# Splitting the q and k projections head by head on ScalarE and VectorE instead of with DMAs, in a fused attention and FP4 feed-forward layer on one core

## The reference

```python
q = split_heads(x @ Wq.T); k = split_heads(x @ Wk.T); v = split_heads(x @ Wv.T)   # x here is layernorm(x)
sim = jnp.einsum('bhid,bhjd->bhij', q, k) * DIM_HEAD ** -0.5
attn = safe_softmax(sim)              # exp(s - max) / (sum + 1e-10)
out = jnp.einsum('bhij,bhjd->bhid', attn, v)
x = x + (out.transpose(0, 2, 1, 3).reshape(B, N, INNER) @ Wo.T + bo)
# feed-forward: both operands of every product are quantised to FP4 in blocks of 16
h = silu(fp4_linear(layernorm(x), w_gate)) * fp4_linear(layernorm(x), w_up)
x = x + fp4_linear(h, w_down)
```

## Time and profile before

| | before |
|---|---|
| median of three runs | 1707.32 us |
| profiled execution, its own time | 1707.32 us |
| its span in the trace | 1705.4 us |
| TensorE (PE) busy | 1529.4 us, 90% |
| VectorE (DVE) busy | 1307.2 us, 77% |
| GpSimd (POOL) busy | 1241.8 us, 73% |
| ScalarE (ACT) busy | 1133.5 us, 66% |
| granted TensorE clock, mean | 0.955 |
| q and k staging DMAs | 384, of 128 KB each, 2.3 to 2.4 us from issue to landing |

### The profile page before, as it was taken

One profiled execution on the slowest core, in us unless ns is written; L12 is line 12 of the kernel. 1 busy time (PEld: TensorE's weight loads), 2 busy tenths in 40 slices (PEclk: granted clock), 3 DMA queues, 4 the chain that ended last, 5 costly groups with the idle time before them and its releaser, 6 DMA issues.

```text
span 1705.4 us, 35322 instructions
## 1 busy us (share of the span) xinstructions
PE 1529.4 (90%) x13828; PEld 1045.6 (61%) x13828; DVE 1307.2 (77%) x2313; ACT 1133.5 (66%) x2094; POOL 1241.8 (73%) x1369
## 2 busy tenths in 40 slices
PE   3898999999899999999999999999999999999965
PEld 2466666666666666666666666666666666666644
DVE  6677876666787788888787887787877887887767
ACT  2577777777676666676666676666676766676633
POOL 3588788888777777777777777777777777777743
PEclk8799999999999999999999999999999999999977
DMA  6110111111111111111110111111111111111000
GB/s 150 38 39 20 35 30 39 37 42 39 30 40 40 38 25 33 25 40 40 39 28 23 32 41 40 39 24 26 33 40 40 38 28 25 29 40 40 2 4 12
DMA packets 46852, 59.77 MB, mean 35 GB/s; under 512 B 8864, under 2 KB 22112, under 8 KB 46688
## 3 DMA queue, kind: packets, MB, share of 16 engines
q1 hardware_dynamic: 46688, 57.52, 14.4%
HBM read 4.80 MB, written 2.10 MB: 4 GB/s over the span
## 4 chain that ended last, share of the span: by engine, by line
PE 66%; DVE 25%; POOL 4%; ACT 3%; issue 2%; DMA 0%; SPq 0%; DVEq 0%; ACTq 0%; POOLq 0%
PE ob L560 19%; PE sm L516 10%; PE st L534 10%; PE st L532 10%; DVE negm L822 6%; PE mb L461 5%; PE mb L477 3%; DVE qv L974 3%; ACT probs L644 2%; POOL p_low L400 2%; DVE q_small L970 2%; PE mb L1073 2%; DVE qv L986 2%; PE mb L466 2%; PE mb L472 2%
## 5 line engine op out<-in xcount | busy, mean ns | idle before, releaser
L400 POOL TENSOR_TENSOR p_low<-probs 128x512 f16<-128x512 f32 x1024 | 1084.8, 1068 | 354.2 <-ACT probs L644 349.3
L644 ACT ACTIVATE probs<-st,lift,exp_scale 128x512 f32<-128x512 f32 x1024 | 793.0, 775 | 312.9 <-PE st L534 292.8
L822 DVE TENSOR_REDUCE negm<-sm 128x1 f32<-128x1024 f32 x512 | 624.0, 1219 | 167.0 <-PE sm L516 166.7
L516 PE MATMUL sm<-k_hh,q_hl 128*128 128x512 f16 x1024 | 316.6, 392 | 100.5 <-DVE negm L822 91.6
L534 PE MATMUL st<-q_hm,k_l 66*128 66x512 f16 x1024 | 400.5, 391 | 0.0
L532 PE MATMUL st<-q_hl,k_hh 128*128 128x512 f16 x1024 | 399.6, 390 | 0.0
L560 PEld LDWEIGHTS ob<-v,p_low 128*128 128x128 f16 x4096 | 283.5, 99 | 129.2 <-issue 10.1
L560 PEld LDWEIGHTS ob<-v,probs 128*128 128x128 bf16 x4096 | 281.8, 99 | 128.9 <-issue 12.1
L560 PE MATMUL ob<-v,p_low 128*128 128x129 f16 x4096 | 325.8, 223 | 2.0 <-POOL p_low L400 2.0
L560 PE MATMUL ob<-v,probs 128*128 128x129 f16 x4096 | 323.0, 222 | 0.2
L658 ACT ACTIVATE oscl<-ob,rden 128x128 f32<-128x128 f32 x512 | 158.0, 363 | 53.5 <-DVE rden L812 53.5
(11 more groups left out here) (157 smaller groups left out, 1560.7 us busy)
## 6 DMA issues: line engine op xcount, KB each, us to landing
k_hh<-k_high SPq DMA_DIRECT2D x128, 128.0 KB, 2.3
k_l<-k_low SPq DMA_DIRECT2D x64, 128.0 KB, 2.3
q_hl<-q_high SPq DMA_DIRECT2D x64, 128.0 KB, 2.3
q_hm<-q_high SPq DMA_DIRECT2D x64, 128.0 KB, 2.4
q_hl<-q_low SPq DMA_DIRECT2D x64, 128.0 KB, 2.4
x<-x SPq DMA_DIRECT2D x4, 512.0 KB, 7.2
q_hm<-m_high SPq DMA_DIRECT2D x128, 1.0 KB
q_hm<-m_low SPq DMA_DIRECT2D x128, 1.0 KB
```

Source lines behind the costliest of these rows:

```text
L400: return pool.tensor_tensor(p_low[b][:, j, :], p, p.bitcast(BF16)[:, 1::2], ALU.subtract)
L516: pe.matmul(sm[:, s % 2, :], q_hl[n][:, t * P:(t + 1) * P], k_hh[n][:, (s % 2) * 512:(s % 2 + 1) * 512], start=True, stop=True).then_inc(s ...
L644: nc.scalar.activation(probs[k % 2][:, s, :], st[s % 2][:, :], ACT.Exp, bias=lift[:, 0:1], scale=exp_scale[:, head, pair:pair + 1]).then_i ...
L822: nc.vector.tensor_reduce(negm[k % 2][:, s // 2:s // 2 + 1], sm[:, :, :].rearrange("p a n -> p (a n)"), AX.X, ALU.max, negate=True).then_i ...
```

## The change

The staging tiles `q_parts` and `k_parts` go. ScalarE writes each head's high part from its 64 rows of the bank straight to its place (`q_hl` or `k_hh`, rows 0 to 63), in two instructions of 64 x 512 where one of 128 x 512 stood. VectorE writes each head's low part straight to its place (`q_hl` rows 64 to 127, or `k_l1` rows 0 to 63), also in two instructions. Four DMAs a round are left: two copy k high to rows 64 to 127 of `k_hh`, and two copy q high to `q_hm`. The first `sm` of the new pair waits for the low parts and for the k copies, and the wait for the q copies stands a round later, at slot 0 of the pair's own scores. The semaphores count eight steps a round in place of four.

```diff
-        q_parts = [sb(f"q_{part}", [P, N], F16) for part in ("high", "low")]
-        k_parts = [sb(f"k_{part}", [P, N], F16) for part in ("high", "low")]
...
-                    wait(sp, s_hi, 4 * g + 2)
+                    wait(sp, s_hi, 8 * g + 4)
                     for h in range(2):
-                        high = k_parts[0][h * DH:(h + 1) * DH, :]
-                        sp.dma_start(k_hh[n + h][0:DH, :], high).then_inc(s_dk, 16)
-                        sp.dma_start(k_hh[n + h][DH:P, :], high).then_inc(s_dk, 16)
-
-                    wait(sp, s_lo, 4 * g + 2)
-                    for h in range(2):
-                        sp.dma_start(k_l1[n + h][0:DH, :], k_parts[1][h * DH:(h + 1) * DH, :]).then_inc(s_dk, 16)
+                        sp.dma_start(k_hh[n + h][DH:P, :], k_hh[n + h][0:DH, :]).then_inc(s_dk, 16)
...
-                    wait(sp, s_hi, 4 * g + 4)
+                    wait(sp, s_hi, 8 * g + 8)
                     for h in range(2):
-                        high = q_parts[0][h * DH:(h + 1) * DH, :]
-                        sp.dma_start(q_hl[n + h][0:DH, :], high).then_inc(s_dq, 16)
-                        sp.dma_start(q_hm[n + h][0:DH, :], high).then_inc(s_dq, 16)
-
-                    wait(sp, s_lo, 4 * g + 4)
-                    for h in range(2):
-                        sp.dma_start(q_hl[n + h][DH:P, :], q_parts[1][h * DH:(h + 1) * DH, :]).then_inc(s_dq, 16)
+                        sp.dma_start(q_hm[n + h][0:DH, :], q_hl[n + h][0:DH, :]).then_inc(s_dq, 16)
...
                         if k == 2 and s == 0:
-                            wait(pe, s_dk, 96 * (g + 1))
-                            wait(pe, s_dq, 96 * (g + 1))
+                            wait(pe, s_lo, 8 * (g + 1))
+                            wait(pe, s_dk, 32 * (g + 1))
...
+                            if slot == 0:
+                                wait(pe, s_dq, 32 * g)
...
-                    nc.scalar.activation(k_parts[0][:, cols], bank[:, :], ACT.Copy,
-                                         scale=k_scale[:, g % PAIRS:g % PAIRS + 1]).then_inc(s_hi, 1)
+                    for h in range(2):
+                        nc.scalar.activation(k_hh[2 * (1 - q) + h][0:DH, cols], bank[h * DH:(h + 1) * DH, :], ACT.Copy,
+                                             scale=k_scale[h * DH:(h + 1) * DH, g % PAIRS:g % PAIRS + 1]).then_inc(s_hi, 1)
...
-                    nc.vector.tensor_tensor(q_parts[1][:, cols], bank[:, :], q_parts[0][:, cols], ALU.subtract
-                                            ).then_inc(s_lo, 1)
+                    for h in range(2):
+                        n = 2 * (1 - q) + h
+                        wait(dve, s_hi, 8 * g + 4 + 2 * c + h + 1)
+                        nc.vector.tensor_tensor(q_hl[n][DH:P, cols], bank[h * DH:(h + 1) * DH, :], q_hl[n][0:DH, cols],
+                                                ALU.subtract).then_inc(s_lo, 1)
...
-                    nc.vector.scalar_tensor_tensor(out=k_parts[1][:, cols], in0=bank[:, :],
-                                                   scalar=k_scale[:, g % PAIRS:g % PAIRS + 1], in1=k_parts[0][:, cols],
-                                                   op0=ALU.mult, op1=ALU.subtract).then_inc(s_lo, 1)
+                    for h in range(2):
+                        n = 2 * (1 - q) + h
+                        wait(dve, s_hi, 8 * g + 2 * c + h + 1)
+                        nc.vector.scalar_tensor_tensor(out=k_l1[n][0:DH, cols], in0=bank[h * DH:(h + 1) * DH, :],
+                                                       scalar=k_scale[h * DH:(h + 1) * DH, g % PAIRS:g % PAIRS + 1],
+                                                       in1=k_hh[n][0:DH, cols], op0=ALU.mult, op1=ALU.subtract
+                                                       ).then_inc(s_lo, 1)
```

More of the change, by code:

```diff
@@ L251, in taken @@
             if name[0] in "qk":
-                return s_lo, 4 * g + (0 if name[0] == "k" else 2) + c + 1
+                return s_lo, 8 * g + (0 if name[0] == "k" else 4) + 2 * c + 2
             if name[0] == "v":
@@ L602, in take @@
                     wait(act, mb_ready[JOBS[m][1]], ready)
-                    nc.scalar.activation(q_parts[0][:, cols], bank[:, :], ACT.Copy).then_inc(s_hi, 1)
+                    for h in range(2):
+                        nc.scalar.activation(q_hl[2 * (1 - q) + h][0:DH, cols], bank[h * DH:(h + 1) * DH, :], ACT.Copy
+                                             ).then_inc(s_hi, 1)
                 elif name[0] == "k":
@@ L771, in take @@
                 if name[0] == "q":
-                    wait(dve, s_hi, 4 * g + 2 + c + 1)
-                    nc.vector.tensor_tensor(q_parts[1][:, cols], bank[:, :], q_parts[0][:, cols], ALU.subtract
-                                            ).then_inc(s_lo, 1)
-                elif name[0] == "k":
-                    wait(dve, s_hi, 4 * g + c + 1)
-                    nc.vector.scalar_tensor_tensor(out=k_parts[1][:, cols], in0=bank[:, :],
-                                                   scalar=k_scale[:, g % PAIRS:g % PAIRS + 1], in1=k_parts[0][:, cols],
-                                                   op0=ALU.mult, op1=ALU.subtract).then_inc(s_lo, 1)
+                    for h in range(2):
[3 more added lines that the diff above has]
+                                                ALU.subtract).then_inc(s_lo, 1)
+                elif name[0] == "k":
+                    for h in range(2):
+                        n = 2 * (1 - q) + h
[4 more added lines that the diff above has]
+                                                       ).then_inc(s_lo, 1)
                 elif name[0] == "m":
```

## The result

The changed kernel takes 1755.04 us (median of 4 runs, 1754.06 to 1755.81) against 1706.46 us for the kernel before on the same chip (4 runs, 1705.01 to 1707.89). The ratio is 1.0284 [1.0268, 1.0299]: 48.6 us slower, where 36.7 us were forecast. In the trace the span grew from 1705.4 to 1755.0 us.

A forecast was written before the change was run, and what follows sets the result against it. TensorE was taken to bound the kernel (busy 90% of the span, 66% of the chain). Terms of 5.4, 4.4, 29.9 and -3 us made +36.7 us on 1707.32: forecast 1744 us, range 1732 to 1756.

The forecast's parts named there:

- The price of a half: On VectorE and ScalarE, 64 x 512 costs what 128 x 512 did, 0.75 or 0.69 us; row changes add 0.12 us.
- Rival A: VectorE's overlap survives the change of rows, so k1 starts only 0.25 us late: +7.5 us, 1715 us; chance 22%.
- rival D: Two halves cost at most 0.4 us more than the whole and round 0 gains 4 us: 1703 us; chance 7%.
- Steps 1 and 2: On TensorE, k1 waits for `m_low`, 0.5 us, and t0 for q0's low part, 0.4 more: 0.9 us a plain round.
- Step 3: Feed-forward rounds: reduction at (1, 1) 1.59 us late past quantisation at (1, 0), score pair waits 0.4 us; 1.3 a round.
- Step 4: Rounds 3 and 4: TensorE already waits for the reduction at (1, 1), so its lateness goes straight through; 2.2 us each.
- step 5: Round 0: the first score pair no longer waits for two q copies and starts earlier; 3 us gained.
- Rival B: New short stops lower the clock of feed-forward rounds by two hundredths more: 23 x 1.0 us on top, 1767 us; chance 10%.
- ScalarE: costed at nothing: ScalarE's added halves, at most 2.8 us a round, are covered by idle time: nothing, or 2.4 us without that cover.
- The moved waits and the DMAs: Later q-copy wait and the wait at (2, 0) cost nothing; removing eight hidden DMAs gives nothing in the steady state.

The follow-up runs named there:

- experiments 9 and 10: Hidden tile's first quantisation piece cut, reciprocal and product moved to (3, 6): first in the kernel before, 1642.39 us; then in the changed kernel, 1707.65 us.
- experiment 7: Kernel before with ScalarE's and VectorE's conversions in halves of 64 x 512 into the staging tiles, all twelve copies kept: 1751.15 us, ratio 1.0272.

## Why the prediction was right, and where its size was off

**The price of a half: right.** 749 and 689 ns, and row changes as taken: `m_low` begins 1.56 us after k0's low part (forecast 1.58), and 0.03 us after the pair's end; in the q pair the reduction begins 1.44 us after (forecast 1.46). The column split shows that it is the change of rows: there the follower begins 0.08 us before the end. The rule of the Trainium skill ("VectorE: DVE Perf Modes", section "Two Vector instructions with no wait between them") says which instructions are held; the trace agrees at each pair: the second half begins 0.03 us after the end of the first, in all 64 pairs of k halves and all 64 of q halves. Rival A is out by this, rival D by the durations.

**Steps 1 and 2: right.** 0.49 us at k1 (forecast 0.5), 0.97 in all (0.9), no further wait in a plain round; taking `m` ahead of k0 removed the first wait, though a plain round got back only 0.18 us of it. Rounds 5 to 8 gave 4.0 us for 3.6.

**Step 3: right place, size off by 1.1 us.** The reduction at (0, 7) was 1.63 us late (forecast 1.59). But the prediction passed this lateness on unchanged through the quantisation at (1, 0): "this one is 1.59 us late". In the traces the reduction at (1, 1) is 2.25 us late. The 0.62 us between are L980, 1331 ns for 712, because it now begins behind GpSimd's `p_low`; the step at (1, 2) adds 0.29. This makes a wait of 0.40 at (1, 2) that was not forecast, and a longer one at (1, 4). From k0's low part the pair at (1, 2) went from 11.43 to 13.01 us and that at (1, 4) from 14.58 to 16.99. With `p_low` cut short the step took 0.52 us, which shows the cause of its length; how much of the price is due to it alone was not isolated. So the term that was mis-sized is 22 x 1.3 = 28.6 us; at full clock it measured 21 x 2.41 and 1.0 for round 9, 51.6.

**Step 4 and step 5: right in size.** Rounds 1 to 4 gave 6.8 us for 6.2: rounds 1 and 2 together 3.0 for 1.8, round 3 1.3 and round 4 2.5 for 2.2 each. Round 0 gave 4.2 for 3. The first score pair began 3.2 us earlier, at 34.84 us (forecast near 34):

```profile
34.84 1.01 PE L502 MATMUL sm<-k_hh,q_hl 128*128 128x512 f16 x2 [2.94 <-DVE q_hl L766]
```

Round 0 took 35.8 us in the kernel before and 33.8 in the first kernel of experiments 9 and 10, whose start is the same, so 4.2 can't be told from 3.

**Rival B: the clock, with the other sign.** A fall lengthens a round by 1.5 to 1.65 us, and the clock fell in 12 of these rounds in place of 20. At full clock they would have grown by 51.6 us, and they grew by 40.0: 11.6 us came back. The forecast of 36.7 us came as near as it did because this return hides half of the error in step 3. That is luck: nothing in the working foresaw it.

**ScalarE: costed at nothing, and that was wrong.** Alone its halves cost 0.46 us a round. On top of VectorE's they cost 0.1 us in a plain round and 1.23 in one with feed-forward at full clock (experiment 7). The prediction held that the exponentials "were ready more than a slot ahead of use". That is so for TensorE, but GpSimd takes them as they come (it waits 349.3 us for them in all before, 402.5 after), and its `p_low`, pushed by 0.75 us, is what the quantisation step then ran into. So the error of step 3 is in the main this term: with VectorE's halves alone the price is 1.01 us, under the 1.3 of the forecast, helped by the second step, which takes 525 ns there for 1245.

**The moved waits and the DMAs: right.** Outside round 0 neither has a row among the waits, and with all copies kept no later round was longer.

## What to carry to other kernels

Two instructions on half the partitions cost twice one on all of them, and a little more for the change of rows; a DMA that is hidden costs nothing, so weigh its removal by what stands in its place. When an engine's work is pushed later, don't only add the delay along its queue: look up what the other engines do at the new moment, since a step that starts just behind a neighbour may take twice as long. Two delays on different engines don't add up either: here each alone cost 0.4% and both 2.7%, because one moved a step and the other its neighbour. And a clock that falls in some rounds hides or feigns a cost: compare rounds at equal granted clock first, then count the falls.

## What was not expected of the hardware

**A VectorE step with three prices.** The same `tensor_tensor` of 128 x 352, both inputs in SBUF, took 0.52 us with GpSimd nearly idle, 0.71 when it began 0.28 us ahead of a `p_low`, and 1.33 when it began 0.09 us behind one. Two patterns hold in all traces but that with `p_low` cut short. A step (L984 or L986, in rounds 10 to 30) that begins while a `p_low` runs ends 0.38 us after that `p_low` does, whether it began 0.01 or 0.89 us behind it; this makes 1.41 us in the worst case and 0.53 in the best. L986 takes 1.25 us in the kernel before for this reason, so some 0.7 us of VectorE's time went there in each such round even before the change. And a step that begins 0.24 to 0.34 us ahead of a `p_low` takes 0.66 to 0.77 us, and the `p_low` 1.32 for 1.04. The Trainium skill ("SBUF — State Buffer", section "SBUF: two separate sides") says that such a VectorE instruction and one of GpSimd take a pair of ports in turn, whichever starts first. The trace agrees where `p_low` is first, since the step's end follows that of `p_low`. Where the step is first, it should keep its 0.52 us by that rule, and it takes 0.71.

**The same wait, with and without a fall of the clock.** The score pair behind the hidden tile's quantisation waits 2.16 us in two neighbouring rounds of the kernel before. In the first its matmuls take 1.03 us, in the second 0.60:

```profile
618.51 1.03 PE L516 MATMUL sm<-k_hh,q_hl 128*128 128x512 f16 x2 [2.16 <-DVE negm L822]
...
669.72 0.60 PE L516 MATMUL sm<-k_hh,q_hl 128*128 128x512 f16 x2 [2.16 <-DVE negm L822]
```

The granted clock of the stretch around each:

```profile
618.00:622.00 4.00, 3.49 (x19) 0.57 0.00 0
669.20:673.20 4.00, 3.48 (x33) 1.00 0.00 0
```

So behind one wait the clock goes to the lower of its two levels (1.2 GHz for 2.4) for most of 4 us, and behind an equal one it doesn't. With this wait cut to 0.56 and 0.20 us it fell in none of rounds 9 to 30. What decides between the two rounds stays open: no run here tells them apart, and why kernels with more short waits had fewer falls wasn't shown either.

**ScalarE seems to hold at a change of rows too.** Its pair of k halves takes 1.39 us in the timeline above, which is 2 x 0.683 and 0.03 between, and `m_high` begins 0.02 us after the pair's end. Before, `m_high` began 0.10 us ahead of the end of the whole conversion. ScalarE's conversion wasn't split by columns, so the change of rows as the cause isn't shown here.
